# TensorE's order of work in a windowed-attention block, and unread products put into its waits in a linear-attention block

## Time and profile before

| what | us |
|---|---|
| median of three runs (7196.7 to 7201.87) | 7199.76 |
| the profiled execution's own time | 7199.84 |
| its span in the trace | 7198.1 |
| TensorE busy | 6417.6 (89%) |
| VectorE busy | 5323.0 (74%) |
| ScalarE busy | 4025.0 (56%) |
| GpSimd busy | 2794.4 (39%) |

### The profile page before, as it was taken

How to read it: one execution, slowest core, us unless ns; L and a number is a source line. 1 busy time by engine, 2 the same in 40 slices (tenths; PEclk the granted TensorE clock), 3 DMA queues, 4 the chain that set the end, 5 groups by cost and what they waited for, 6 DMA issues and landing times. The chain is left out here.

```text
span 7198.1 us, 187818 instructions
## 1 busy us (share of the span) xinstructions
PE 6417.6 (89%) x74368; PEld 3935.9 (55%) x74368; DVE 5323.0 (74%) x8918; ACT 4025.0 (56%) x5988; POOL 2794.4 (39%) x1672
## 2 busy tenths in 40 slices
PE   7989987887797999989999789989899999989999
PEld 5767665443432333333333256666577777766677
DVE  7867577665556999999999856677577777768544
ACT  4556343665446777777777645555244444456433
POOL 3311175332215888888888501165022222222000
PEclk9999978998898999999999989999999999999999
DMA  1000000000101222222222100010000000000000
GB/s 29 0 22 12 6 9 8 3 4 2 16 1 56 76 74 76 73 81 77 76 77 76 49 12 13 9 32 3 12 2 2 2 2 2 2 15 14 8 9 9
DMA packets 115168, 188.62 MB, mean 26 GB/s; under 512 B 38293, under 2 KB 74330, under 8 KB 114266
## 3 DMA queue, kind: packets, MB, share of 16 engines
q1 hardware_dynamic: 111514, 182.22, 7.9%
q10 hardware_dynamic: 3264, 0.54, 0.1%
HBM read 172.74 MB, written 7.86 MB: 25 GB/s over the span
## 5 line engine op out<-in xcount | busy, mean ns | idle before, releaser
L2624 POOL TENSOR_TENSOR m_dBx<-m_dtx,m_Bs 128x1024 f32<-128x1024 f32 x512 | 1159.4, 2284 | 229.5 <-DVE m_hs L3002 182.7
L3002 DVE TENSOR_TENSOR_SCAN m_hs<-m_ps_dA,m_dBx 128x512 f32<-128x512 f32 x1024 | 1193.6, 1207 | 55.2 <-POOL m_dBx L2624 53.6
L2749 PE MATMUL m_ps_y<-m_yc,ident 128*128 128x512 f32 x2048 | 1015.1, 618 | 0.0
L2859 ACT ACTIVATE m_ps_dA<-m_dt,m_A 128x504 f32<-128x504 f32 x1024 | 678.7, 678 | 440.5 <-DVE m_hs L3002 438.0
L2122 POOL TENSOR_TENSOR a_s<-a_s,a_den 128x1024 f32<-128x1024 f32 x128 | 243.7, 1904 | 1111.8 <-DVE a_den L2168 1111.8
L3013 DVE TENSOR_TENSOR m_yc<-m_hs,m_ps_C 128x1024 f32<-128x1024 f32 x512 | 612.7, 1197 | 1.1 <-PE m_ps_C L2730 1.1
L2749 PEld LDWEIGHTS m_ps_y<-m_yc,ident 128*128 128x128 f32 x2048 | 348.1, 189 | 355.6 <-issue 355.3
L2730 PE MATMUL m_ps_C<-m_parts,m_sel 48*128 48x512 bf16 x512 | 198.2, 387 | 182.8 <-DVE m_yc L3013 182.8
L2730 PEld LDWEIGHTS m_ps_C<-m_parts,m_sel 48*128 48x128 bf16 x512 | 47.3, 92 | 571.7 <-DVE m_yc L3013 432.5
L636 POOL TENSOR_TENSOR c_kbd<-c_kf,c_hmask 128x1024 f32<-128x1024 f32 x66 | 125.0, 1895 | 502.0 <-ACT c_kf L545 483.9
L2166 DVE TENSOR_REDUCE a_den<-a_s 128x16 f32<-128x1024 f32 x128 | 156.0, 1219 | 203.9 <-ACT a_s L2073 203.9
(11 more groups left out here) (748 smaller groups left out, 15771.7 us busy)
## 6 DMA issues: line engine op xcount, KB each, us to landing
m_Bs<-BC_rows SPq DMA_DIRECT2D x256, 512.0 KB, 3.5
c_kvb<-in_ctxT SPq DMA_DIRECT2D x68, 128.0 KB, 2.1
c_kvb<-in_ctxT SPq DMA_DIRECT2D x17, 256.0 KB, 2.6
out_dram<-X SPq DMA_DIRECT2D x16, 256.0 KB, 2.3
BC_rows<-m_low SPq DMA_DIRECT2D x32, 64.0 KB, 2.8
part_rows<-m_split SPq DMA_DIRECT2D x32, 48.0 KB, 1.7
m_parts<-part_rows SPq DMA_DIRECT2D x32, 48.0 KB, 1.7
c_table<-in_table SPq DMA_DIRECT2D x2, 512.0 KB, 3.4
```

The costliest lines, as they stand in the source:

```text
L2624: return nc.gpsimd.tensor_tensor(to, one, other, ALU.mult)
L2749: last = nc.tensor.matmul(ps_y[:, m, :], C.ident[:], of[:, m, :], start=s == 0, stop=s == NS - 1)
L2859: nc.scalar.activation(seqs(ps_dA[:, h % 3, :]), seqs(dt[:, par, m, :]), ACT.Exp, scale=A[:, second, m, s:s + 1]).then_inc(decay, 1)
L3002: nc.vector.tensor_tensor_scan(hs[:, s % HS, m, :], ps_dA[:, (2 * s + m) % 3, :], dBx[:, s % BX, m, :], 0.0, ALU.mult, ALU.add).then_inc(s ...
```

## The change

In linear attention, a new helper writes float32 products of the identity by itself into the unused columns of ps_c, which nothing reads. They are put at six places ahead of the loop, and four of them into each slot from slot 1 on, ahead of `turn_output`, behind a wait for on_ready. In focus attention TensorE's and ScalarE's lists are put in another order, and the exponentials are made in two instructions of 1024 columns, the second behind the logarithm and exponential of the variances.

```diff
+def fill_wait(C, bank, times):
+    for _ in range(times):
+        C.nc.tensor.matmul(bank[:, 0:P], C.ident[:], C.ident[:], start=True, stop=True)
...
+        unread = ps_c[:, UT * NH * VW:512]
...
             nc.tensor.matmul(ps_s[0:32, 0, 0:D], wcT[:], we[:], start=True, stop=True).then_inc(folded, 1)
+            fill_wait(C, unread, 2)
             pe.wait_ge(read, 1)
...
+            fill_wait(C, unread, 3)
             pe.wait_ge(prepared, n_prepared)
...
                 scores(w + 1, 1 - u)
                 if weigh:
+                    pe.wait_ge(on_ready, w)
+                    fill_wait(C, unread, 4)
                     if project:
                         pe.wait_ge(out_read, w - 1)
                     turn_output(w - 1)
...
             turn_rows(0, 0, True)
+            fill_wait(C, unread, 2)
             queries_keys(0, 0)
             values(0, 0, True)
+            fill_wait(C, unread, 2)
             turn_rows(1, 1)
+            fill_wait(C, unread, 2)
             queries_keys(1, 1)
+            fill_wait(C, unread, 5)
             turn_rows(2, 0)
...
                 if r == 0:
-                    pe.wait_ge(exped, j + 1)
+                    pe.wait_ge(exped, 2 * j + 2)
                     pe.wait_ge(v_taken, 2 * j + 2)
...
                 for t in range(N + 1):
                     j = first + t
+                    if t + 2 < N:
+                        pe.wait_ge(var_read, j + 2)
+                        project(ph, t + 2)
                     if t < N:
                         scores(ph, t)
                     if t:
-                        turn_probs(ph, t - 1, 0)
-                        turn_probs(ph, t - 1, 1)
-                    if t + 2 < N:
-                        pe.wait_ge(var_read, j + 2)
-                        project(ph, t + 2)
-                    if t:
-                        turn_probs(ph, t - 1, 2)
-                        turn_probs(ph, t - 1, 3)
-                        weigh(ph, t - 1)
+                        for r in range(RG):
+                            turn_probs(ph, t - 1, r)
                     if t + 2 < N:
                         carry(ph, t + 2)
-                    if t < N:
-                        spread_values(ph, t)
+                    if t:
+                        weigh(ph, t - 1)
                     if t + 2 < N:
                         pe.wait_ge(kv_taken, j + 3)
                         variances(ph, t + 2)
                     if t + 1 < N:
                         masks(ph, t + 1)
+                    if t < N:
+                        spread_values(ph, t)
...
-            def exponents(ph, n):
+            def exponents(ph, n, half):
                 j, _, _ = job(ph, n)
-                act.wait_ge(scores_read, j + 1)
-                nc.scalar.activation(s1[:, j % 2, :, :], s1[:, j % 2, :, :], ACT.Exp).then_inc(exped, 1)
+                if half == 0:
+                    act.wait_ge(scores_read, j + 1)
+                at = s1[:, j % 2, 2 * half:2 * half + 2, :]
+                nc.scalar.activation(at, at, ACT.Exp).then_inc(exped, 1)
...
                 for t in range(N + 1):
-                    if t:
-                        take_probs(ph, t - 1, (0, 1))
                     if t + 2 < N:
                         take_qk(ph, t + 2)
                     if t:
-                        take_probs(ph, t - 1, (2, 3))
+                        take_probs(ph, t - 1)
+                    if t + 2 < N:
+                        take_kv(ph, t + 2)
                     if t < N:
-                        exponents(ph, t)
+                        exponents(ph, t, 0)
                     if t:
                         denominators(ph, t - 1)
                     if t + 2 < N:
-                        take_kv(ph, t + 2)
-                    if t < N:
-                        take_values(ph, t)
-                    if t + 2 < N:
                         spreads(ph, t + 2)
                         inverse_spreads()
+                    if t < N:
+                        exponents(ph, t, 1)
+                        take_values(ph, t)
```

More of the change, by code:

```diff
@@ L3661, in inverse_spreads, with take_probs @@
                 nc.scalar.activation(spread[:], spread[:], ACT.Exp, scale=-0.5).then_inc(spread_ready, 1)
-            def exponents(ph, n):
+            def exponents(ph, n, half):
                 j, _, _ = job(ph, n)
-                act.wait_ge(scores_read, j + 1)
-                nc.scalar.activation(s1[:, j % 2, :, :], s1[:, j % 2, :, :], ACT.Exp).then_inc(exped, 1)
-            def take_probs(ph, n, turns):
+                if half == 0:
+                    act.wait_ge(scores_read, j + 1)
+                at = s1[:, j % 2, 2 * half:2 * half + 2, :]
+                nc.scalar.activation(at, at, ACT.Exp).then_inc(exped, 1)
+            def take_probs(ph, n):
                 j, _, _ = job(ph, n)
@@ L3671, in take_probs @@
                     act.wait_ge(out_done, j)
-                for r in turns:
+                for r in range(RG):
                     act.wait_ge(pT_done, 4 * j + r + 1)
```

## The result

| | us |
|---|---|
| before, median of 4 runs (7189.03 to 7201.87) | 7198.23 |
| after, median of 4 runs (7129.98 to 7139.84) | 7134.23 |
| ratio, with its 95% interval | 0.9914 [0.9902, 0.9927] |
| forecast | 7135 |
| profiled execution after: its own time, its span | 7129.98, 7128.2 |

The account below looks back on a forecast made before the run. Linear attention was taken as bound by VectorE's list at 2.4 GHz and TensorE's at 1.2 GHz, focus attention by TensorE's list. 7199.84 - 16 (linear) - 49 (focus) = 7135, its own range 7118 to 7150.

Parts of the forecast that it names:

- The clock stays up: Linear attention: TensorE's clock holds from the third slot on; 31 periods take 240.1 us, 20.8 less.
- The products lie in the wait at no cost: Linear attention slots: four products fit the wait before turn_output, 0 a slot at the high clock, 0.3 as upper end.
- I charge 3 us: Linear attention, slots 0 and 1: still at the low clock, with little wait for the products; 3 us added.
- I charge 1.5: Linear attention's opening: sixteen added products partly outlast its short waits; 1.5 us added, between 0 and 4.
- Rival 1: Linear attention: the clock doesn't hold, falls stay and some ten low slots are 2 longer; 7172, chance 0.11.
- The start: Focus attention, each phase's start: project(2) comes ahead of the first scores with a logarithm wait; 2.8 later, twice.
- The first and the last turns give 2 x 3.8 back: Focus attention: each phase's first and last turns lack project or its waits, giving 2 x 3.8 us back.
- The whole turn, 14.80 to 13.55: Focus attention: 13.04 of work plus a 0.5 wait at turn_probs 2; 1.25 less a turn, 18 turns, 22.5 us.
- 2.2 less: Focus attention, turns of a phase's last iteration: 14.80 to 12.6 as carry has values alone; 12 turns, 26.4 us.
- part of that fell into the 1.76 and will now show: +2: Focus attention: TensorE's stops with nothing awaited, partly inside the old waits of 1.76 a turn, now show; 2 us added.
- rival 4: Focus attention: a shorter turn meets more stops without a releaser, eight of 2 us more; 7151, chance 0.08.
- Rivals 2 and 3: Focus attention: ScalarE paces turns at 14.2, 7155, chance 0.11; or turn_probs 0 waits for ScalarE's long chain, 7224, chance 0.04.

Follow-up runs that it names:

- linear alone: Products in linear attention as in the change, focus attention as in the kernel before; 7165.54 against 7196.13, ratio 0.9958.
- the split carry: Changed kernel with carry in two, its keys' product between turn_probs 1 and 2, its values' product ahead of weigh; 7145.97 against 7138.12 for the changed kernel.
- the whole exponentials: Changed kernel with a job's exponentials in one instruction of 2048 columns at the place of the first half; 7177.13 against 7198.42 before.
- the shifted one: Changed kernel with carry in two halves, plus sixteen more unread products after linear attention's last projection to shift the code; 7150.53 against 7200.99 before.

## Why the prediction was right in sum, and where its steps were wrong

The forecast was 7135 by -16 and -49; the first pair of traces has -24.1 and -42.5, the second -20.5 and -33.2, with 3.3 and 7.9 from the rest of the program. The mechanisms named for both blocks show in the traces, but that the sum holds to 1 us is luck: linear attention gave 4 to 8 more than forecast, focus attention 6.5 to 16 less, and of what it gave 13 to 21 us came with no change in its code (below).

*Linear attention.*

- The clock stays up: right, 1.00 from 930 to 1160. The price of the falls, 20.8 over 31 periods, was met in the first trace (260.9 to 240.1); the second has 243.5.
- The products lie in the wait at no cost: right. There was even more room than the 1.07, as eight products showed, so that the upper end of 0.3 a slot was too cautious.
- "I charge 3 us" for slots 0 and 1: 0 in the first trace and 3.4 in the second, where the clock fell in the second period. "I charge 1.5" for the opening: too much. Up to the first mask the granted clock is 0.79 with the opening's products and 0.53 without, and the mask comes 0.8 earlier; the second comes 0.7 later. At worst they cost 0.4 (272.4 against 272.0 without them). The tail, from the last mask to the last product, was not in the sum at all: 12.8 and 12.9 in place of 15.3 and 15.2. From periods, opening and tail the linear block gave -20.8 - 0.8 - 2.5 = -24.1, and -17.4 - 0.8 - 2.3 = -20.5.
- Rival 1 (7172) did not come. The rule of the Trainium skill on which it rested ("TensorE: Matmul & The Clock Gate", section "HAM oscillation — how this bites in real kernels") would have the products change nothing, since no wait was as long as the gap that it names (from the first to the last mask of the kernel before the longest was 2.2). The runs disagree: 262.2 us with the wait and no products, 242.3 with one product, 240.1 and 243.5 with four, and no other difference between them.

*Focus attention.* A block of two phases can be split by the reduces of VectorE. From the first to the last of each phase, phase one fell from 359.3 (second trace 351.3) to 327.7 (325.6), phase two from 168.8 (170.8) to 151.0 (158.6): -49.4, and -37.9. The rest of the block, starts and ends, grew by 6.9 and 4.7.

- The start: the first reduce came 2.9 and 2.7 later (forecast 2.8), twice 2.8 is 5.6 against 6.9 and 4.7. Right.
- "The first and the last turns give 2 x 3.8 back": wrong, and the largest miss of the first trace. From scores to scores the first turn of each phase fell from 12.0 to 10.7. The last one had 13.0 and 13.3 before, and has 15.1 and 12.7 (in the second traces 12.7 and 13.0, then 13.9 and 13.8). All four together gave 1.1 and 0.6 in place of 7.6.
- The whole turn, 14.80 to 13.55: right for the turns that are not disturbed (13.5), and wait for wait: turn_probs 2 starts 1.40 after number 0, as worked out, and nothing waits at weigh. But the median went from 15.0 to 14.1, just under the 14.2 that I had named as the sign of being wrong; the mean over phase one is 14.25 (327.7 over 23). Two scores of the changed kernel show one reason that recurs:

```profile
1344.84 2.35 PE L3461 MATMUL x_ps_s<-x_kbd,x_qs 32*32 32x128 f32 x128
...
1358.87 1.91 PE L3461 MATMUL x_ps_s<-x_kbd,x_qs 32*32 32x128 f32 x128
```

  The same 128 records take 1.91 or 2.35, with nothing awaited. From their start to that of the next line the 36 scores have a median of 1.83 before and 2.07 after, in sum 74.0 before (73.9 in the second trace and with linear alone) and 82.0 after (85.1): 8 to 11 us that the forecast didn't have, in a line that the change didn't touch.
- The last iteration's turn, "2.2 less": too much. 12.9 was the best and 13.4 the median, against 12.6. In sum, stops included, the twelve gave 22.1 and 14.2 of the 26.4, the eighteen whole ones 26.3 and 24.5 where 22.5 was forecast. But linear alone, with the old lists, has its eighteen whole turns in 271.5 us in place of 288.9 and 283.1 and its twelve last ones in 188.5 in place of 185.8. Against it the new order gave 8.9 and 12.9 in the whole turns and 24.8 and 16.9 in the last ones: at equal code ahead, the 22.5 of the whole turns is the term that came out at about half. A turn of the last iteration in the changed kernel:

```profile
1517.65 1.29 PE L3472 MATMUL x_ps_t<-ident,x_vals 128*32 128x32 f32 x128 [0.18 <-DVE x_even L3961]
...
1521.69 1.52 PE L3461 MATMUL x_ps_s<-x_kbd,x_qs 32*32 32x128 f32 x101 [0.43 <-issue]
```

  With carry shorter, spread_values comes earlier against the output that it waits for (0.18), and a stop of 0.43 lies in the scores, where the old order had waits behind it that could take such a stop in. 12 turns of 0.8 are 9.6 us, of which the stops in the scores are a part.
- "part of that fell into the 1.76 and will now show: +2": too small. The long stops (over 1.2 us) grew from 15.5 and 13.6 us to 19.2 and 21.2, all stops from 20.3 and 17.8 to 25.5 and 27.7. In the eight other traces with the new lists or variants of them the long ones take 21.3 to 33.6, in the four with the old lists or carry moved alone 7.6 to 15.5. How far the stops are more, and how far a wait no longer hides them, the profile doesn't tell. That is rival 4 in part, at about half its price of 16; with a turn of 13.0 (the split carry) it took all that the turn had won, and more.
- Rivals 2 and 3 did not come: no turn but the last of each phase waits at turn_probs 0 (1.6, as before), and ScalarE's halves are ready in time. How thin that is, the whole exponentials show: 0.84 and 0.47 at spread_values, and 43 us.

How much of the 42.5 belongs to the new order can be told only at equal code ahead of it. Linear attention as before: 744.0 and 736.6 to 709.3, -35 and -27. Linear attention as after: 723.2 to 701.5 and 703.4, -22 and -20. So the order itself is worth 20 to 35, not 49, and 13 to 21 us of the focus block's 42.5 came without any change in its code. That share was in no term of the sum, and I had no rows for it. Kernels with equal lists spread by as much: seven traces have exactly the new lists, behind linear attention in six versions, and their focus blocks take 701.5 to 715.3. I had also named a change of over 5 us behind the two blocks as a sign of being wrong. It was 4.8 in the first pair and 7.2 in the second; over all the kernels, with the same code there, that part takes 5252 to 5263.

## What to carry to other kernels

Where TensorE has slack in a short period and its clock falls, put an unread product into the wait, behind the semaphore that proves the wait exists; one of 0.27 us was enough here, and four cost nothing, but count the room before taking more. Moves in an engine's list are to be judged as a set: carry ahead of weigh alone made the program slower than before, and the whole set without the split exponentials left the focus block where it was. Before a few us are put down to an edit, take a second trace and compare it with a kernel that has the same code ahead of the place; here the same kernel differed by 3.4 us in one block and the same lists by 14 in another.

## What the runs showed of the hardware that I had not expected

**Stops that belong to the code's place.** The kernel before, TensorE, one stop:

```profile
1448.89 1.27 PE L3456 MATMUL x_ps_t<-ident,x_vals 128*32 128x32 f32 x126 [0.21 <-DVE x_odd L3946]
1452.86 0.27 PE L3456 MATMUL x_ps_t<-ident,x_vals 128*32 128x32 f32 x2 [2.70 <-issue]
```

and the DMA queues from 1449.0 to 1453.5 (packets, MB, share of 16 engines):

```profile
q8 instruction: 1, 0.02, 1.3%
```

There is one packet of instructions, 16 KB, that starts at 1450.5; the stop starts at 1450.2. That alone says little, for the block has 121 such packets, one every 4 to 5 us within the phases, and most come without a stop. In the version with the split carry four stops in a row begin at 1315.3, 1358.5, 1404.3 and 1450.1 and four packets at 1315.2, 1358.5, 1404.5 and 1450.0. The same kernel has its stops at nearly the same places in two traces (before: near 1404, 1450, 1790 and 1885 both times), and kernels whose code differs ahead of the block have them elsewhere and in other number: 7 and 6 of over 1.2 us for before, 6 for the linear part alone, 10 and 11 for the changed kernel, 16 for the shifted one. The traces of one kernel are not alike in all of it: a stop near 1309 stands in the first of before alone, one near 1399 in the first of the changed kernel alone. That TensorE waits for instructions in them fits all of this, and isn't shown. Whether a shorter turn runs out of instructions more often by itself, or the place alone decides, isn't settled: 13.0 a turn had 14 and 16 stops, 13.5 had 10 to 13, 14.8 (the old lists) 6 and 7, 17.3 (carry alone) 4, but 14.6 (whole exponentials) had 13.

A stop costs more than its own length. Behind this one, with the columns of the earlier trace rows:

```profile
1452.00:1458.80 6.80, 5.94 (x88) 2.72 (x95) 1.36 (x2) 3.02 (x4) 0.00 (x0) 0.50 0.01 2
```

```profile
1453.06 3.78 PE L3425 MATMUL x_ps_a<-x_square,x_mean 128*128 128x512 f32 x4
```

The clock was 1.00 from 1443 to 1450 and is 0.50 here, and the variances take 3.78 in place of 1.98. From weigh to weigh this turn takes 20.3 us, 5.5 more than the 14.80, for a stop of 2.70. Over all the traces the clock falls behind 73 of the 87 stops of over 2 us inside the phases. It is also where linear alone differs from before: the granted clock of its focus block is 0.95 against 0.93 and 0.94.

**VectorE beside GpSimd.** The scaling of the queries, in the kernel before and in the changed one:

```profile
1367.04 1.89 DVE L3913 TENSOR_SCALAR x_qs<-x_qk,x_g_q,x_be_q 128x512 f32<-128x512 f32 x1
```

```profile
1309.85 0.54 DVE L3928 TENSOR_SCALAR x_qs<-x_qk,x_g_q,x_be_q 128x512 f32<-128x512 f32 x1
```

and GpSimd's square in the kernel before:

```profile
1366.74 1.89 POOL L3778 TENSOR_TENSOR x_square<-x_qk 128x1024 f32<-128x1024 f32 x1 [1.65 <-ACT x_qk L3643]
```

The same instruction takes 0.54 in place of 1.89. Before, 32 of the 36 overlapped with the square, took 1.05 to 2.10 and ended 0.28 behind it; the four that did not overlap took 0.54. In the new order GpSimd is idle at that time, and 34 take 0.54. The Trainium skill has this ("SBUF — State Buffer", section "Who interferes with whom"): the two engines share a pair of ports, which one holds for a whole instruction. The trace agrees, by 1.35 us. In the focus block VectorE is busy for 398.15 us in place of 440.10. No wait of TensorE names this line in either kernel, so there is no sign that it brought any time.
